# Decoder blends ahead of the waits on ScalarE: the multiply stage's last twelve steps and the second write's first part

## The reference, cut to what matters

```
gate = g_in @ mlp_in_w[0].T                  # g_in, u_in: 1024 tokens x 256; 1024 outputs
up   = u_in @ mlp_in_w[1].T
mlp_out = silu(gate) * up                    # "multiply stage"
hidden  = rat_write(hidden, mlp_out, ...)    # "second write": o_d, A_B = mlp_out @ weights; softplus, exp, update
x = x + hidden
idx = sum(bit p of qweight << p, p = 0..3)   # 1024 x 1024 codes of 4 bits
w   = take_along_axis(lut4, idx)             # decoded weights, 16 values a row
x = x + layernorm(x) @ w.T + bias            # "last product"
```

## Time and profile before

| | us |
|---|---|
| median of 3 runs | 1802.63 (1797.2 to 1807.58) |
| the profiled execution's own time | 1792.48 |
| its span | 1790.7 |
| PE busy | 1586.8 (89%) |
| DVE busy | 1356.7 (76%) |
| ACT busy | 914.7 (51%) |
| steps 4 to 15 of the multiply stage | 1542.7 to 1592.3 |
| its last decoder keep ends | 1598.0 |
| second write's first part, to `soft(0)` | 1598.3 to 1637.1 |
| last product's 16 units | 1667.8 to 1787.6 |

### The profile page before, as it was taken

How to read it: one execution, slowest core, us unless ns; L and a number is a source line. 1 busy time by engine, 2 the same in 40 slices (tenths; PEclk the granted TensorE clock), 3 DMA queues, 4 the chain that set the end, 5 groups by cost and what they waited for, 6 DMA issues and landing times. The chain is left out here.

```text
span 1790.7 us, 21054 instructions
## 1 busy us (share of the span) xinstructions
PE 1586.8 (89%) x6880; PEld 1046.3 (58%) x6880; DVE 1356.7 (76%) x2078; ACT 914.7 (51%) x1686; POOL 578.1 (32%) x463
## 2 busy tenths in 40 slices
PE   4899999999999999999999988767899767888999
PEld 3466666666666666666666655465455446445444
DVE  7688788788788788788788867586578578678881
ACT  3345455455455455455554453233458776567630
POOL 2246346446446446446446444210110100000000
PEclk9999999999999999999999999979889855898999
DMA  5001101101102102101101000050634200000121
GB/s 183 24 25 59 36 25 59 36 24 59 36 24 59 36 24 59 36 25 59 36 24 48 24 25 23 18 190 37 129 74 69 91 1 1 1 36 1 47 77 41
DMA packets 30963, 84.20 MB, mean 47 GB/s; under 512 B 6006, under 2 KB 7304, under 8 KB 30600
## 3 DMA queue, kind: packets, MB, share of 16 engines
q1 hardware_dynamic: 30856, 82.87, 15.8%
HBM read 70.27 MB, written 12.58 MB: 46 GB/s over the span
## 5 line engine op out<-in xcount | busy, mean ns | idle before, releaser
L518 DVE SCALAR_TENSOR_TENSOR acc<-pj,sc_o,acc 128x1024 f32<-128x1024 f32 x232 | 293.8, 1278 | 89.4 <-PE pj L649 86.1
L628 POOL TENSOR_TENSOR prob<-prob,inv_total 128x512 f32<-128x512 f32 (+3 forms) x256 | 189.6, 745 | 385.4 <-DVE inv_total L560 385.4
L518 DVE SCALAR_TENSOR_TENSOR q_acc<-pj,sc_q,q_acc 128x1024 f32<-128x1024 f32 x224 | 286.2, 1278 | 34.5 <-PE pj L649 29.3
L649 PE MATMUL pj<-ctx_hi,w_o 128*128 128x512 f32 x528 | 237.1, 449 | 25.5 <-ACT spare L407 12.3
L649 PE MATMUL pj<-zT_hi,w_q 128*128 128x512 f32 x512 | 225.6, 441 | 4.0 <-PEq L81 3.1
L649 PE MATMUL pj<-ctx_lo,w_o 128*128 128x512 f32 x528 | 207.9, 394 | 0.0
L461 ACT ACTIVATE prob<-ps,low_max 128x512 f32<-128x512 f32 (+3 forms) x256 | 134.1, 526 | 144.4 <-DVE low_max L553 144.3
L649 PE MATMUL pj<-zT_lo,w_q 128*128 128x512 f32 x512 | 204.5, 399 | 0.0
L703 PE MATMUL ps<-kT,qT 128*128 128x512 f32 (+3 forms) x512 | 185.7, 445 | 10.5 <-ACT prob L461 10.5
L727 PE MATMUL pv<-probT,v 128*128 128x512 f32 (+3 forms) x512 | 169.5, 433 | 0.0
L649 PEld LDWEIGHTS pj<-ctx_hi,w_o 128*128 128x128 f32 x528 | 99.1, 188 | 110.5 <-DVE acc L518 43.0
(11 more groups left out here) (338 smaller groups left out, 3141.0 us busy)
## 6 DMA issues: line engine op xcount, KB each, us to landing
raw_o<-in_w_o SPq DMA_DIRECT2D x33, 512.0 KB, 3.6
raw_q<-in_w_q SPq DMA_DIRECT2D x32, 512.0 KB, 3.6
x_ring<-qk_kept SPq DMA_DIRECT2D x64, 128.0 KB, 5.1
ln_x<-in_x SPq DMA_DIRECT2D x8, 512.0 KB, 6.9
raw_kv<-in_w_k SPq DMA_DIRECT2D x8, 512.0 KB, 3.6
raw_kv<-in_w_v SPq DMA_DIRECT2D x8, 512.0 KB, 4.6
x<-in_x SPq DMA_DIRECT2D x8, 512.0 KB, 6.6
x_kept<-x SPq DMA_DIRECT2D x8, 512.0 KB, 2.9
```

The source lines that it names most:

```text
L518: dve.scalar_tensor_tensor(out=dst, in0=pj[slot][:], scalar=scale, in1=dst, op0=ALU.mult, op1=ALU.add).then_inc(evac_v, 1)
L628: pool.tensor_tensor(prob[:, k % PROBS, 0:w], prob[:, k % PROBS, 0:w], inv_total[:, n:n + 1].to_broadcast([P, w]), ALU.mult).then_inc(norm ...
L649: ins = pe.matmul(pj[slot][:, b * S:(b + 1) * S], lhs, part[:, b * S:(b + 1) * S], start=n == 0, stop=n == 1)
```

## The change: blends first

In the multiply stage's steps 4 to 15 ACT's list had the copies of the turned halves (steps 9 and 14), the silu, and then the blends of the step. Now the blends stand first, then the copies, then the silu. In the second write's loop the blends of an iteration stood last, and now stand first. Nothing else is changed: the number of instructions, the lists of PE, DVE, POOL and SP, the tiles and all semaphores are the same.

```
             for n in range(MLP_IN_READ, len(STEPS)):
+                for q in range(mlp_quarter(n), mlp_quarter(n + 1)):
+                    deq.blend(act, q)
                 if n in MLP_TURNS:
                     deq.copy(act, MLP_TURNS[n], p_w, fT)
                 gated(n)
-                for q in range(mlp_quarter(n), mlp_quarter(n + 1)):
-                    deq.blend(act, q)
...
             for i in range(half + 3):
+                for q in range(w2_quarter(i), w2_quarter(i + 1)):
+                    deq.blend(act, q)
                 if 1 <= i <= half:
                     wr.copy_od(act, i - 1)
...
                 if i - 1 in W2_TURNS[0]:
                     half_tile(W2_TURNS[0][i - 1])
-                for q in range(w2_quarter(i), w2_quarter(i + 1)):
-                    deq.blend(act, q)
```

## The result

| | before | after |
|---|---|---|
| median of 11 runs each, us | 1800.81 (1796.13 to 1807.58) | 1812.12 (1807.66 to 1819.94) |
| ratio, 95% interval | | 1.0076 (1.006 to 1.0093) |
| profiled execution, span | 1790.7 | 1818.2 |
| step 4's first matmul | 1542.73 | 1556.60 |
| from there to the second write's start | 55.60 | 70.12 |

What follows compares the result with a forecast made beforehand. PE, busy without a pause to the last product, was taken to bound the kernel, so unit 0's start sets the end. Multiply stage +15.3 and second write -0.7 gave +14.6 us on 1802.63, 1817 us, range 1805 to 1823.

Steps and rivals of the forecast that it cites:

- What bounds: End of the kernel: PE runs the 16 units to the end, so moving unit 0's start moves the end by as much.
- ACT and DVE take turns: Multiply stage: silus wait for blends that wait for DVE behind the previous silu; steps 10 to 13 cost +4.0 us.
- The copies: Turns ahead of steps 9 and 14: half-turn copies wait behind four blends and a lowest bit, +4.2 and +2.7 us.
- The clock: PE behind its two new gaps: lower clock costs 2.6 us each, +0.9 and +2.6 against before.
- the clock costs nothing: Rival: no clock loss behind the multiply stage's new gaps, stage +10.1, whole +9.3, 1812 us; chance 0.08.
- The tail: End of the multiply stage: last silu to last keep 4.3 us where it was 5.8, -1.5 us.
- The second write: Second write: six blends still precede copy_low(3), soft(0) comes 5.0 us earlier, unit 0 gains only -0.7 us.
- Which engine holds unit 0: Second write: unit 0 waits for PE, whose work from main(4) to unit 0 takes 35.2 us.
- the second write pays in full: Rival: unit 0 follows DVE, so the second write gains 5.0 us, whole +10.3, 1813 us; chance 0.08.
- The rival of the other side: Rival: multiply-stage half-turn copies not held back, only the second write counts, -0.7 to -5.0 us, say 1800; chance 0.14.
- The forecast of 1817: Whole kernel: +14.6 us on the median shown, 1802.63, giving 1817 us, +0.8%.

Runs made afterwards that it cites:

- the other ten steps: Kernel before with the new order only in the ten multiply-stage steps other than 9 and 14: ratio 1.0037, +6.7 us.
- the filled gaps: Changed kernel plus 6 and 9 unused matmuls on PE between the half turns ahead of steps 9 and 14: ratio 1.0067 to before, +12.0 us.
- the multiply part alone: Kernel before with only the multiply stage in the new order, second write in the old: ratio 1.0075, +13.5 us.
- the write part alone: Kernel before with only the second write in the new order, multiply stage in the old: ratio 0.9993, -1.3 us.
- the hybrid: Kernel before with the second write's blends first in iterations 0 to 4 and last in iteration 5: ratio 0.9975, -4.5 us.
- the run with both: Kernel before with half-turn copies ahead of blends in steps 8 and 13, and second-write blends first except in iteration 5: ratio 0.9938, -11.2 us.
- The bit made a quarter earlier: Multiply stage in the new order, second write in the old, DVE making the next half's lowest bit one quarter earlier: ratio 1.0057 to before, +10.3 us.
- the run with the copies first: Kernel before with the multiply stage ordered copies, blends, silu, second write in the old order: ratio 1.0043, +7.7 us.

## Why the prediction was right

- **What bounds.** Unit 0 to the end was 122.88 before and stayed 122.9 to 123.9 us in eleven of the twelve new profiles and 122.4 in the other, whatever happened before it: what moves unit 0 moves the end.
- **ACT and DVE take turns.** The silus from 9 on were to be 5.9, 4.4, 4.7 and 2.7 apart, and are 5.93, 4.43, 4.60 and 2.70. The run with the other ten steps, where the copies stand in front as before, shows that it costs by itself.
- **The copies.** First copy +4.2, measured +4.1; gaps of 6.4 and of 8 to 9, measured 6.26 and 8.75. Second copy 4.6 behind silu 13, measured 4.59.
- **The clock.** Taken at 2.6 for each gap. Measured from copy to silu, less 4.75 at the full clock: 7.70 and 6.39, that is 2.95 and 1.64. The sum, 4.6, was forecast 0.6 too high, which is the largest part of the error of the stage (15.3 for 14.5); the filled gaps, another way to it, give 3.8 to 4.5. Against before, whose first gap had cost 1.7 and whose second nothing, the clock adds 1.3 and 1.6 us where the forecast had +0.9 and +2.6: one too low and one too high, so that part of the fit of the sum is luck. The lower clock was to last 5 to 6 us behind each gap; it did so behind the first, and under 3.9 behind the second. In the profile of the multiply part alone the same two losses are 1.3 and 2.5: which gap pays more changes from run to run. The rival *the clock costs nothing* fell with it. The Trainium skill ("TensorE: Matmul & The Clock Gate", Part 1: The HAM clock gate) puts the ramp penalty, that of the matmuls before the clock is released, under 1% of a typical kernel's span. The 4.5 us are 0.25% of 1812, so the trace agrees with the bound; but the 2.9 us that the clock adds to what before loses are a fifth of the difference that was asked for.
- **The tail.** 4.3 from last silu to last keep, measured 4.1.
- **The second write.** -0.7 forecast, of which the text has a source for 0.5; -1.3 in the profile of after, of which 0.5 is `main(0)` at 7.41 for 7.89 us, by the clock (granted 0.71 for 0.67 over it); -0.6 in the write part alone up to unit 0, and -0.1 to its end. `soft(0)` came 5.0 earlier in after, as forecast, and 4.5 in the write part alone, and as good as nothing of it arrives. That the six blends in front of `copy_low(3)` are the reason was argued before and is shown by the hybrid, which takes them away and has 4.5 us.
- **Which engine holds unit 0** was read wrong in one point. The forecast took the 35.2 us from `main(4)` to unit 0 for PE's. In the kernel before it is DVE's chain behind the softplus that comes last, and PE's chain has ended 0.3 us earlier, as ACT shows, two instructions ahead of unit 0:
```profile
1666.41 0.30 ACT L2254 ACTIVATE f_sd<-f_mv,eps 128x1 f32<-128x1 f32 x1 [0.30 <-DVE f_mv L2350]
```
  Two distances say the same in all profiles. From the first abs to unit 0 it is 30.74 to 30.79 us wherever the second write is in the old order or in the hybrid's, however long `main(4)` was. With the new order it is 34.4 to 34.7, and there the distance from `main(4)` to unit 0, less `main(4)` itself, is 27.08 to 27.09: PE holds it. So the rival *the second write pays in full* was right that unit 0 follows DVE, and wrong in the price, since PE's chain, only 0.3 us shorter, takes over. The sum comes out: 0.5 by the earlier `main(4)`, 0.3 by this slack, less 0.3 of clock in `main(4)` (8.11 for 7.84 us), is the 0.6 of the write part alone. In the hybrid DVE's chain is last again, so that the 1.7 us of clock that `main(4)` has back in the run with both bring unit 0 nothing (30.74 from the first abs in either).
- **The rival of the other side** needed the lowest bit of half 9 over 4 us earlier. The bit made a quarter earlier brings 1.7 us per gap; no run brought the 4, so that its price stays unmeasured.
- **The forecast of 1817** is 5 us above the measured median. 1.8 of these come from the base, whose median was 1802.63 of 3 runs and is 1800.81 of 11; 0.9 from the difference, 13.7 for 14.6; and 2.4 from the scatter of the medians, which are 11.3 apart and not 13.7.

## What to carry to other kernels

Work that fills an engine's wait belongs in front of it only if it can itself start then; a blend that waits for VectorE drags everything behind it on ScalarE's list, and when that is what VectorE waits for, the two engines take turns and the lead is gone. Before moving work ahead of a copy, look at who waits for that copy and whether that engine is the bound: here TensorE, which pays for the gap a second time by its clock. A short copy for which the bounding engine waits belongs in front of the filler, in either order. And what one engine gains ahead of a point where several chains meet counts only up to the next chain: here the softplus came 4.5 us earlier in the write part alone and unit 0 came 0.6 earlier, since TensorE's chain was only 0.3 us shorter than VectorE's.

## What was not expected of the hardware

The stretch between 1100 us and step 4, the same instructions in all kernels, lasted from 442.7 us in the profile of before to 456.6 in that of after, 444 to 454 in the others, with the granted clock at 0.83 and 0.80 in the two ends. A single profile of this kernel can differ from another by 14 us, as much as the change, in work that the change does not touch. And behind a gap of nearly the same length, 2.14 to 2.17 us, the clock fell in some places and not in others: 1.11 and 0.66 us for the half turn in the earlier trace rows, 1.12 in the run with the copies first and 0.66 in that with the other ten steps, both at the first turn with 2.17. In the hybrid of the second write it fell with no gap at all: PE had been busy for 20 us without a pause when `main(4)` began at 1634.62, and the granted clock was 0.51 from 1634.7 to 1638.0. So a wait of PE is one way to lose the clock here, and not the only one.
